# Scan inputs and output stage of a state-space network on Trainium2: the deltas by another route, and a longer pipeline

## The chip, the cores and the metric

The kernel runs on one core of one Trainium2 chip. The metric is the device time of one execution in microseconds (us). Three runs of the kernel before took 20491.51, 20492.61 and 20494.03 us; the median is 20492.61. A separate execution was recorded by the hardware profiler, and all rows in this document come from it.

## The reference

The program maps 32 images of 96 channels and 32 x 32 points (1024 points, HW below) through four layers. The change touches layers 0 and 1, both selective scans. From an inner signal u of 192 channels (in layer 1 four directions of it, 768 channels) a projection gives B and C (16 rows each) and a low-rank dt (6 rows), and dt gives a step size delta for every channel and point:

```python
x_dbl = xl @ W_x
dt_r = x_dbl[..., :dr]
Bm = x_dbl[..., dr:dr + n]
Cm = x_dbl[..., dr + n:]
delta = jax.nn.softplus(dt_r @ W_delta + b_delta)
...
dA = jnp.exp(dt[:, :, None] * A)
h = dA * h + (dt * u_t)[:, :, None] * B_t[:, None, :]
```

Layer 0 does the same forward and backward along sequences of 8 frames, with u made by a causal convolution of four taps and a SiLU. It then adds both directions, multiplies by a gate z, projects back to 96 channels, adds the input and normalises over the channels. Layers 2 and 3 (attention and a quantised feed-forward) are as they were.

## The kernel before, in words

The program is a row of stages with a barrier between them. Each stage is a function with its own buffers; it reads its inputs from HBM and writes its results there. Within a stage each engine has its own program, written out in the code, and runs it strictly in that order; semaphores say when an operand is ready. `nth(k)` is the value that a semaphore has once step k is done. `turns` unrolls four turns in a loop. So the order of the code is the order of the work, and a wait at the head of an engine holds everything behind it. Three functions matter.

`l0_scan_inputs` (line 292, run forward as `l0pf` and backward as `l0pb`) prepares the scans of layer 0. A turn handles two frames in three tiles of 128 rows by 1024 points. VectorE makes u by four taps (lines 415 and 419), TensorE projects u to 38 rows (`project`, lines 501 and 502), ScalarE copies them out (`read`, line 528), TensorE makes the deltas' argument x = W dt + b in PSUM tile `pd` (`deltas`, lines 487 and 490). The softplus is computed as max(x, 0) + ln(1 + exp(-|x|)): VectorE stores max(x, 0) in `dl` (line 437) and -|x| = x - 2 max(x, 0) in `ab` (line 440), ScalarE takes exponential and logarithm (546, 548), and GpSimd adds (line 391). A turn later VectorE multiplies delta by u (line 427), TensorE transposes the product in 8 blocks (466), and ScalarE copies that out (537). At the end of a turn ScalarE applies the SiLU, which needs another table (559, 540).

`l0_out_proj` (line 570, `l0out`) takes the images in pairs. For a pair, each step is done for both images before the next: VectorE adds the directions (624) and multiplies by z (629), TensorE projects (664), VectorE adds the input (636), TensorE averages (672), VectorE subtracts (642), ScalarE squares (694), TensorE averages (678), ScalarE takes logarithm and exponential (698, 702), VectorE scales and shifts (647, 650). All input buffers are double. SP loads image k once image k - 2 is out of its buffers, ScalarE's queue stores.

`l1_scan_inputs` (line 1148, `l1p`) does for layer 1 what the first function does for layer 0, an image a turn, in six tiles (three forward, three reversed). There is no convolution. The projection is one block of eight f32 matmuls of 512 columns in the second slot of a turn (`project`, line 1292), for the next image; deltas run two tiles ahead (1299), the product with u runs three tiles behind on VectorE (1271), the transposes four (1308), the copy out five (1354).

In the names of rows, `px` is the projection in PSUM, `dts` its copy, `pt` the transposed product and `dut` its copy, `bt` the transposed B.

Of the kernel before, what the change touches and what calls it, by code (L numbers as in the profile page):

```python
# [19 lines left out]
BF16 = mybir.dt.bfloat16  # L20
# [271 lines left out]
def l0_scan_inputs(nc, back, xmp, w, us, dls, duts, bts, crows, ident):  # L292
# [8 lines left out]

    with ExitStack() as stack:
# [19 lines left out]
        const, taps, conv, silu, xd, dtc, btm, btc, dtm, plus, absd, expd, lnd, sumd, dud, dutm, dutc, passed = r.step_sems(  # L322
            "const", "taps", "conv", "silu", "xd", "dtc", "btm", "btc", "dtm", "plus", "absd", "expd", "lnd", "sumd",
# [9 lines left out]
        with nc.Block() as block:  # L333
# [52 lines left out]
            @block.gpsimd  # L386
            def _(pool):
                def turn(k, s):
                    for t in range(T):
                        pool.wait_ge(lnd, nth(T * k + t))  # L390
                        pool.tensor_tensor(dl[:, s % 2, t, :], dl[:, s % 2, t, :], ln[:, t, :], ALU.add).then_inc(sumd, 1)

                turns(pool, turn, 0, 0, UNROLL, ITEMS)

            @block.vector
            def _(dve):
# [4 lines left out]
                def turn(k, s):  # L401
# [50 lines left out]
            def _(pe):  # L452
# [3 lines left out]
                def turn(k, s):  # L456
# [2289 lines left out]
```

## Time and profile before

| | |
|---|---|
| median of three runs | 20492.61 us |
| profiled execution | 20482.76 us |
| its span, first to last instruction | 20481.2 us |
| granted TensorE clock, mean over the span | 0.957 |
| TensorE matmul busy | 18308.0 us, 89% |
| VectorE busy | 17098.0 us, 83% |
| ScalarE busy | 15840.3 us, 77% |
| GpSimd busy | 13907.5 us, 68% |

The shares are averages over stages with different limits, so they do not tell what a change in one stage is worth. PE is TensorE (PEld its weight loads), DVE is VectorE, ACT is ScalarE, POOL is GpSimd, SP the engine that issues most DMAs.
### The profile page before, as it was taken

Reading aid. Unit: us, or ns where it says so; the run is one execution under the profiler, and the core shown is the slowest. Engines: PE = TensorE matmul, PEld = TensorE weight load, DVE = VectorE, ACT = ScalarE, POOL = GpSimd, SP = SyncE. Lnnn points to the kernel's source line nnn. Section 1 sums busy time; section 2 is a strip of 40 time slices with the busy share of each in tenths; the row PEclk is TensorE's granted clock in tenths of the full one; section 3 lists DMA queues with packets and bytes.
Section 4 is the critical chain, followed back from the end, with each engine's and each line's share of the span. In section 5 each row is a group of like instructions: output and inputs, shape, how many; then the busy total and the mean of one; then the engine's idle time right before and its main releaser. Section 6 shows DMA issues by size and latency. Waiting matters only on the chain. (4 is left out here: it accounts for less than half of the span.)

```text
span 20481.2 us, 269190 instructions
## 1 busy us (share of the span) xinstructions
PE 18308.0 (89%) x75272; PEld 10298.6 (50%) x75272; DVE 17098.0 (83%) x12555; ACT 15840.3 (77%) x24692; POOL 13907.5 (68%) x6884
## 2 busy tenths in 40 slices
PE   8799997999958899889899999999999999789798
PEld 3355553555523344335566666666666665245353
DVE  4899998899967499469899999999999999755666
ACT  7599995999934555567799999999999999234545
POOL 0399992899916488155599999999999999000101
PEclk9799997999989999999999999999999999799999
DMA  5688875888873411657633333333333333910303
GB/s 176 204 241 241 237 230 190 244 241 241 243 209 87 174 72 69 210 205 266 232 128 117 126 117 127 117 127 116 127 117 127 116 127 106 217 42 27 91 28 85
DMA packets 842574, 3172.29 MB, mean 155 GB/s; under 512 B 101542, under 2 KB 124682, under 8 KB 816140
## 3 DMA queue, kind: packets, MB, share of 16 engines
q1 hardware_dynamic: 820236, 3080.90, 47.0%
q10 hardware_dynamic: 20992, 75.51, 1.0%
q8 instruction: 593, 9.72, 0.2%
q14 instruction: 753, 6.17, 0.1%
HBM read 2317.15 MB, written 838.88 MB: 154 GB/s over the span
## 5 line engine op out<-in xcount | busy, mean ns | idle before, releaser
L1575 DVE TENSOR_TENSOR_SCAN l1s_h<-l1s_da,l1s_pd 128x1024 f32<-128x1024 f32 x3072 | 6818.6, 2273 | 329.2 <-PE l1s_pd L1510 246.3
L1613 ACT ACTIVATE l1s_dm<-l1s_dut,l1s_bt 128x384 f32<-128x384 f32 x7680 | 4182.5, 602 | 16.7 <-PE l1s_pd L1510 16.5
L1596 ACT ACTIVATE l1s_da<-l1s_dl,l1s_a 128x1024 f32<-128x1024 f32 x3072 | 3493.3, 1137 | 75.1 <-DVE l1s_h L1575 51.0
L1510 PE MATMUL l1s_pd<-l1s_id,l1s_dm 128*128 128x128 f32 x23040 | 3059.0, 275 | 159.9 <-DVE l1s_h L1575 116.1
L1510 PEld LDWEIGHTS l1s_pd<-l1s_id,l1s_dm 128*128 128x128 f32 x23040 | 2632.3, 142 | 826.8 <-issue 533.1
L1479 POOL TENSOR_TENSOR l1s_sm<-l1s_h 128x1024 f32<-128x1024 f32 x1024 | 2434.2, 2377 | 170.4 <-DVE l1s_h L1575 170.2
L1484 POOL TENSOR_TENSOR l1s_pb<-l1s_h,l1s_cc 128x1024 f32<-128x1024 f32 x1024 | 2436.5, 2379 | 1.0 <-DVE l1s_h L1575 0.3
L1488 POOL TENSOR_TENSOR l1s_pa<-l1s_sm,l1s_cc 128x1024 f32<-128x1024 f32 x1024 | 2433.6, 2377 | 0.0
L886 POOL TENSOR_TENSOR dw_acc<-dw_acc,dw_prod 128x961 f32<-128x961 f32 (+3 forms) x704 | 1573.2, 2281 | 1005.7 <-ACT dw_prod L839 997.5
L1520 PE MATMUL l1s_py<-l1s_pb,l1s_id 128*128 128x512 f32 x4096 | 2014.3, 614 | 215.2 <-POOL l1s_pb L1484 214.8
L2145 POOL CAST ffn_h<-ffn_z 128x1024 fp8e5<-128x1024 f16 x128 | 181.0, 1415 | 2894.7 <-DVE ffn_z L2165 2889.6
L1520 PE MATMUL l1s_py<-l1s_pa,l1s_id 128*128 128x512 f32 x4096 | 1927.4, 593 | 0.3 <-POOL l1s_pa L1488 0.3
L2400 POOL TENSOR_TENSOR l0sf_pr<-l0sf_h,l0sf_cc 128x1024 f32<-128x1024 f32 x768 | 1816.6, 2386 | 69.1 <-DVE l0sf_h L2482 51.1
L2400 POOL TENSOR_TENSOR l0sb_pr<-l0sb_h,l0sb_cc 128x1024 f32<-128x1024 f32 x768 | 1813.7, 2380 | 67.4 <-DVE l0sb_h L2482 60.6
L817 PE MATMUL dw_pc<-dw_vol,dw_diag 128*128 128x512 f32 (+7 forms) x4224 | 1765.1, 581 | 57.2 <-DMA dw_vol<-n 30.3
L916 DVE SCALAR_TENSOR_TENSOR dw_pc<-dw_vol,dw_wt,dw_pc 128x961 f32<-128x961 f32 (+5 forms) x1280 | 1484.6, 1234 | 210.0 <-PE dw_pc L817 206.0
L2438 PE MATMUL l0sf_py<-l0sf_pr,l0sf_id 128*128 128x512 f32 x3072 | 1578.6, 596 | 0.0
L2438 PE MATMUL l0sb_py<-l0sb_pr,l0sb_id 128*128 128x512 f32 x3072 | 1578.6, 596 | 0.0
L2530 ACT ACTIVATE l0sb_dm<-l0sb_dut,l0sb_bt 128x192 f32<-128x192 f32 x3584 | 1313.9, 443 | 9.4 <-DMA l0sb_dl<-l0dlsb 9.4
L2530 ACT ACTIVATE l0sf_dm<-l0sf_dut,l0sf_bt 128x192 f32<-128x192 f32 x3584 | 1312.1, 441 | 9.2 <-DMA l0sf_dl<-l0dlsf 9.2
L817 PEld LDWEIGHTS dw_pc<-dw_vol,dw_diag 128*128 128x128 f32 (+1 forms) x4224 | 774.8, 184 | 1047.6 <-issue 1031.3
L2418 PEld LDWEIGHTS l0sb_pd<-l0sb_id,l0sb_dm 128*128 128x128 f32 x6144 | 761.7, 142 | 929.3 <-issue 682.4
(300 smaller groups left out, 32080.3 us busy)
## 6 DMA issues: line engine op xcount, KB each, us to landing
l1s_cc<-crows SPq DMA_DIRECT2D x1024, 512.0 KB, 3.7
l0sf_cc<-l0crowsf SPq DMA_DIRECT2D x512, 512.0 KB, 5.8
l0sb_cc<-l0crowsb SPq DMA_DIRECT2D x512, 512.0 KB, 5.4
l0sf_cc<-l0crowsf SPq DMA_DIRECT2D x512, 256.0 KB, 7.7
l0sb_cc<-l0crowsb SPq DMA_DIRECT2D x512, 256.0 KB, 7.1
dls<-l1p_dl SPq DMA_DIRECT2D x192, 512.0 KB, 7.0
duts<-l1p_dut SPq DMA_DIRECT2D x64, 1536.0 KB, 5.8
l1s_dut<-duts SPq DMA_DIRECT2D x64, 1536.0 KB, 7.2
```

What stands on the lines that cost most here:

```text
L817: mm = pe.matmul(pixels(pc[:, f % 4, :])[:, ys, xs], diag[:, v % tiles, diag_taps.index(tap), :], source(v, f, tap, ys, xs), start=(n == 0 ...
L1479: pool.tensor_tensor(sm[:, rnd % 2, :], h[:, rnd * HT % 4, :], h[:, (rnd * HT + 1) % 4, :], ALU.add)\
L1484: pool.tensor_tensor(pb[:, rnd % 2, :], h[:, (rnd * HT + 2) % 4, :], cc[:, rnd % 4, :], ALU.mult)\
L1488: pool.tensor_tensor(pa[:, rnd % 2, :], sm[:, rnd % 2, :], cc[:, rnd % 4, :], ALU.mult)\
L1510: mm = pe.transpose(pd[:, s % 2, blk * 128:blk * 128 + 128], dm[:, rnd % 2, blk, j * 128:j * 128 + 128], idt[:, :])
L1520: mm = pe.matmul(target[:, hs], idt[:, :], prods[:, rnd % 2, hs], start=(n == 0), stop=(n == N - 1))
L1575: dve.tensor_tensor_scan(h[:, s % 4, :], da[:, j, :], pd[:, s % 2, :], 0.0, ALU.mult, ALU.add)\
L1596: act.activation(da[:, j, :], dl[:, half, j, :], ACT.Exp, scale=a[:, HT * half + j, n:n + 1])\
L1613: ins = act.activation(dm[:, rnd % 2, blk, :], dut[:, half, blk, :], ACT.Identity, scale=bt[:, half, blk, n:n + 1])
L2400: pool.tensor_tensor(pr[:, s % 4, :], h[:, s % 6, :], cc[:, rnd % 4, j, :], ALU.mult).then_inc(prod, 1)
L2438: mm = pe.matmul(py[:, j, HALVES[half]], idt[:, :], pr[:, s % 4, HALVES[half]], start=(n == 0), stop=(n == N - 1))
L2530: ins = act.activation(out, src, ACT.Identity, scale=b)
```

## The change

**Layer 0, scan inputs.** GpSimd's program is gone. VectorE computes -|x| in one operation, by setting the sign bit of x in PSUM, and no longer stores max(x, 0). The new last step `softplus` reads x again from PSUM and ln(1 + exp(-|x|)) from SBUF and gives max(x, 0) + ln(...) in one operation. It comes after the convolution tap of its slot, and the sign operation before the tap. TensorE makes the deltas one tile ahead. A buffer of `pd` is now free only once `softplus` has read it.

**Layer 0, output stage.** Input buffers are four deep, the stores are on SP, and the three parts of an image's chain are done in three successive turns, each engine working on images k, k + 1 and k + 2 in a turn.

**Layer 1, scan inputs.** The dt rows of the projection are made nine times (three groups of three copies); 128 output rows were computed before too, most of them zeros. ScalarE copies all 128 rows to bf16 (`parts`), VectorE subtracts to get what is left for 64 rows (`rest`), ScalarE rounds that to bf16, VectorE subtracts once more for 32 rows. So `parts` holds high, middle and low parts of dt, and W is split in three in the same way; one bf16 matmul with 128 rows of contraction gives the sum of the nine products. A bf16 row of ones adds the bias row by two more matmuls an image. B and C are copied apart (`bc`). The projection is in four pieces, spread over four slots. The product with u moves to GpSimd, the softplus is as in layer 0, and both VectorE operations on deltas are in two halves of 512 points with a semaphore step each.

```diff
 # l0_scan_inputs
-            @block.gpsimd
-            def _(pool):
-                def turn(k, s):
-                    for t in range(T):
-                        pool.wait_ge(lnd, nth(T * k + t))
-                        pool.tensor_tensor(dl[:, s % 2, t, :], dl[:, s % 2, t, :], ln[:, t, :], ALU.add).then_inc(sumd, 1)
...
+                            dve.wait_ge(dtm, nth(T * k + t))
+                            dve.wait_ge(expd, nth(T * (k - 1) + t))
+                            dve.tensor_scalar(ab[:, t, :].bitcast(I32), pd[:, (s + t) % 2, :].bitcast(I32), SIGN, None, ALU.bitwise_or).then_inc(absd, 1)
...
+                            dve.wait_ge(lnd, nth(T * k + t))
+                            dve.scalar_tensor_tensor(out=dl[:, p, t, :], in0=pd[:, (s + t) % 2, :], scalar=0.0, in1=ln[:, t, :],
+                                                     op0=ALU.max, op1=ALU.add).then_inc(sumd, 1)
...
                     for t in range(T):
                         times_u(t)
+                        minus_abs(t)
                         convolve(t)
-                        minus_abs(t)
+                        softplus(t)
                     convolve(3)
...
-                        pe.wait_ge(absd, nth(T * k + t - 2))
+                        pe.wait_ge(sumd, nth(T * k + t - 2))
...
                     for t in range(T):
+                        if t < T - 1:
+                            deltas(k, s, t + 1)
+                        else:
+                            deltas(k + 1, s + 1, 0)
                         turn_du(t)
-                        deltas(t)
                         if t < 2:
                             project(t)
 # l0_out_proj, VectorE
-                with dve.Fori(0, FRAMES) as c:
-                    for pair in pairs:
...
+                    if there(k1):
+                        dve.wait_ge(proj, nth(k1))
+                        dve.wait_ge(s_xm[s1 % 2], (k1 - s1 % 2) * 8)
+                        dve.tensor_tensor(xo[:, s1 % 2, :], xin[:, s1, :], po[:, s1 % 2, :], ALU.add).then_inc(resid, 1)
+                    if there(k2):
+                        dve.wait_ge(s_in[s2], c2 * 112 + 112)
...
 # l1_scan_inputs, GpSimd
+                            pool.wait_ge(sumd, nth(2 * q + 1))
+                            pool.wait_ge(dutm, nth(q - 2))
+                            pool.tensor_tensor(du[:, t % 2, :], dl[:, t, :], in_order(s, t), ALU.mult).then_inc(dud, 1)
 # VectorE
+                            for i, hs in enumerate(HALVES):
+                                dve.wait_ge(dtm, nth(2 * q + i))
+                                dve.tensor_scalar(ab[:, t % 3, hs].bitcast(I32), pd[:, t % 2, hs].bitcast(I32), SIGN, None,
+                                                  ALU.bitwise_or).then_inc(absd, 1)
...
+                        if t == 3 and there(k + 1):
+                            dve.wait_ge(hi, nth(k + 1))
+                            dve.wait_ge(mid, nth(k))
+                            dve.tensor_tensor(rest[GROUPS, :], px[GROUPS, :], parts[GROUPS, p, :], ALU.subtract).then_inc(res, 1)
+                        if t == 4 and there(k + 1):
+                            dve.wait_ge(mid, nth(k + 1))
+                            dve.tensor_tensor(parts[96:128, p, :], rest[96:128, :], parts[96:128, p, :], ALU.subtract)\
+                               .then_inc(lo, 1)
 # TensorE
+                        pe.wait_ge(lo, nth(m))
+                        for i, hs in enumerate(HALVES):
+                            pe.wait_ge(sumd, nth(2 * (T * m + v - 2) + i))
+                            mm = pe.matmul(pd[:, v % 2, hs], wdel[:, v, :], parts[:, (s + (t + 2) // T) % 2, hs],
 # ScalarE
+                        if t == 3 and there(k + 1):
+                            act.wait_ge(xd, nth(k + 1))
+                            act.wait_ge(dtm, nth(2 * (T * (k - 1) + T - 1) + 1))
+                            act.activation(parts[:, p, :], px[:, :], ACT.Copy).then_inc(hi, 1)
+                        if t == 4 and there(k + 1):
+                            act.wait_ge(res, nth(k + 1))
+                            act.activation(parts[GROUPS, p, :], rest[GROUPS, :], ACT.Copy).then_inc(mid, 1)
```

The order of TensorE's instructions in layer 1's scan inputs, before, from one image's projection on (`px` is the projection, `pt` the transposes, `pd` the deltas):

```order
L1292 MATMUL l1p_px<-l1p_u,l1p_wsum 128x512 x8
L1308 MATMUL l1p_pt<-l1p_id,l1p_du 128x128 x8
L1299 MATMUL l1p_pd<-l1p_dts,l1p_wd 128x512 x2
L1308 MATMUL l1p_pt<-l1p_id,l1p_du 128x128 x8
L1299 MATMUL l1p_pd<-l1p_dts,l1p_wd 128x512 x2
L1314 MATMUL l1p_px<-l1p_id,l1p_dts 128x16 x8
L1308 MATMUL l1p_pt<-l1p_id,l1p_du 128x128 x8
L1299 MATMUL l1p_pd<-l1p_dts,l1p_wd 128x512 x2
```

And after, from the deltas ahead of the second projection piece on:

```order
L1348 MATMUL l1p_pd<-l1p_parts,l1p_wdel 128x512 x2
L1357 MATMUL l1p_pt<-l1p_id,l1p_du 128x128 x8
L1338 MATMUL l1p_px<-l1p_u,l1p_wsum 128x512 x2
L1340 MATMUL l1p_px<-l1p_one,l1p_oneat 128x512
L1348 MATMUL l1p_pd<-l1p_parts,l1p_wdel 128x512 x2
L1357 MATMUL l1p_pt<-l1p_id,l1p_du 128x128 x8
L1338 MATMUL l1p_px<-l1p_u,l1p_wsum 128x512 x2
L1348 MATMUL l1p_pd<-l1p_parts,l1p_wdel 128x512 x2
L1357 MATMUL l1p_pt<-l1p_id,l1p_du 128x128 x8
L1338 MATMUL l1p_px<-l1p_u,l1p_wsum 128x512 x2
L1340 MATMUL l1p_px<-l1p_one,l1p_oneat 128x512
L1348 MATMUL l1p_pd<-l1p_parts,l1p_wdel 128x512 x2
```

The eight projection matmuls stood in one row; now two of them stand behind each of four transposes, and the deltas come ahead of the transposes.

ScalarE in the same stage, before, from the copy of the projection on (`dut` is the copy of the transposes, the two `ln` rows are exponential and logarithm):

```order
L1346 ACTIVATE l1p_dts<-l1p_px 38x1024
L1354 ACTIVATE l1p_dut<-l1p_pt 128x8x128
L1360 ACTIVATE l1p_ln<-l1p_ab 128x1024
L1362 ACTIVATE l1p_ln<-l1p_ln 128x1024
L1354 ACTIVATE l1p_dut<-l1p_pt 128x8x128
L1360 ACTIVATE l1p_ln<-l1p_ab 128x1024
L1362 ACTIVATE l1p_ln<-l1p_ln 128x1024
L1368 ACTIVATE l1p_bt<-l1p_px 128x128
```

And after, from the copy out ahead of that copy on:

```order
L1398 ACTIVATE l1p_dut<-l1p_pt 128x8x128
L1402 ACTIVATE l1p_parts<-l1p_px 128x1024
L1410 ACTIVATE l1p_ln<-l1p_ab 128x1024
L1412 ACTIVATE l1p_ln<-l1p_ln 128x1024
L1416 ACTIVATE l1p_bc<-l1p_px 32x1024
L1398 ACTIVATE l1p_dut<-l1p_pt 128x8x128
L1405 ACTIVATE l1p_parts<-l1p_rest 64x1024
L1410 ACTIVATE l1p_ln<-l1p_ab 128x1024
L1412 ACTIVATE l1p_ln<-l1p_ln 128x1024
L1398 ACTIVATE l1p_dut<-l1p_pt 128x8x128
L1410 ACTIVATE l1p_ln<-l1p_ab 128x1024
```

Three instructions of 1024 points stand where one stood, and the copy of B and C comes after the first tile's logarithm.

VectorE in layer 0's forward scan inputs, before, from the second slot's product on (`du` is the product with u, `u` the taps):

```order
L427 TENSOR_TENSOR l0pf_du<-l0pf_dl,l0pf_u 128x1024
L419 SCALAR_TENSOR_TENSOR l0pf_u<-l0pf_xb,l0pf_cw,l0pf_u 128x1024 x3
L437 TENSOR_SCALAR l0pf_dl<-l0pf_pd 128x1024
L440 SCALAR_TENSOR_TENSOR l0pf_ab<-l0pf_dl,l0pf_pd 128x1024
L427 TENSOR_TENSOR l0pf_du<-l0pf_dl,l0pf_u 128x1024
L419 SCALAR_TENSOR_TENSOR l0pf_u<-l0pf_xb,l0pf_cw,l0pf_u 128x1024 x3
L437 TENSOR_SCALAR l0pf_dl<-l0pf_pd 128x1024
L440 SCALAR_TENSOR_TENSOR l0pf_ab<-l0pf_dl,l0pf_pd 128x1024
L419 SCALAR_TENSOR_TENSOR l0pf_u<-l0pf_xb,l0pf_cw,l0pf_u 128x1024 x3
```

And after, from the same product on:

```order
L419 TENSOR_TENSOR l0pf_du<-l0pf_dl,l0pf_u 128x1024
L427 TENSOR_SCALAR l0pf_ab<-l0pf_pd 128x1024
L411 SCALAR_TENSOR_TENSOR l0pf_u<-l0pf_xb,l0pf_cw,l0pf_u 128x1024 x3
L435 SCALAR_TENSOR_TENSOR l0pf_dl<-l0pf_pd,l0pf_ln 128x1024
L419 TENSOR_TENSOR l0pf_du<-l0pf_dl,l0pf_u 128x1024
L427 TENSOR_SCALAR l0pf_ab<-l0pf_pd 128x1024
L411 SCALAR_TENSOR_TENSOR l0pf_u<-l0pf_xb,l0pf_cw,l0pf_u 128x1024 x3
L435 SCALAR_TENSOR_TENSOR l0pf_dl<-l0pf_pd,l0pf_ln 128x1024
L411 SCALAR_TENSOR_TENSOR l0pf_u<-l0pf_xb,l0pf_cw,l0pf_u 128x1024 x3
```

The sign operation (`ab`) has moved ahead of the taps, and what gives `dl` now reads `ln` and stands behind them.

## Rows read from the trace of the kernel before

**Rows 1.** Busy time by window, core 0: three changed stages, columns as in the first line
```profile
core 0: us, PE busy (x) PEld busy (x) DVE busy (x) ACT busy (x) POOL busy (x), PEclk, DMA share, GB/s
363.00:944.00 581.00, 385.19 (x1408) 195.36 (x1408) 473.47 (x340) 270.98 (x244) 112.55 (x48) 0.75 0.56 185
5725.00:6265.00 540.00, 276.93 (x512) 92.48 (x512) 288.58 (x260) 99.60 (x96) 0.00 (x0) 0.77 0.74 213
9187.00:10115.00 928.00, 806.79 (x3328) 460.80 (x3328) 787.94 (x587) 621.07 (x642) 456.85 (x192) 0.97 0.70 264
```

**Rows 2.** Timeline of VectorE, one turn, first layer: start us, us, engine, line
```profile
598.70 3.37 DVE L419 SCALAR_TENSOR_TENSOR l0pf_u<-l0pf_xb,l0pf_cw,l0pf_u 128x1024 f32<-128x1024 f32 x1
601.99 1.21 DVE L427 TENSOR_TENSOR l0pf_du<-l0pf_dl,l0pf_u 128x1024 f32<-128x1024 f32 x1
603.13 2.25 DVE L415 TENSOR_SCALAR l0pf_u<-l0pf_xb,l0pf_cw 128x1024 f32<-128x1024 f32 x3
607.71 1.23 DVE L437 TENSOR_SCALAR l0pf_dl<-l0pf_pd 128x1024 f32<-128x1024 f32 x1 [2.33 <-PE l0pf_pd L487]
...
611.24 5.84 DVE L419 SCALAR_TENSOR_TENSOR l0pf_u<-l0pf_xb,l0pf_cw,l0pf_u 128x1024 f32<-128x1024 f32 x3
```

**Rows 3.** Line 419, the convolution taps: duration ns min/median/max
```profile
L419 DVE SCALAR_TENSOR_TENSOR l0pf_u<-l0pf_xb,l0pf_cw,l0pf_u x144: 1269/1279/3452, 378.3 to 862.3; 128x1024 f32<-128x1024 f32 x144
```

**Rows 4.** Timeline of ScalarE in the same turn, and five turns later
```profile
602.10 2.77 ACT L559 ACTIVATE l0pf_u<-l0pf_u 128x3072 f32<-128x3072 f32 x1 [1.96 <-DVE l0pf_u L419]
606.18 1.02 ACT L537 ACTIVATE l0pf_dut<-l0pf_pt 128x1024 f32<-128x1024 f32 x1
...
766.69 2.77 ACT L559 ACTIVATE l0pf_u<-l0pf_u 128x3072 f32<-128x3072 f32 x1 [1.96 <-DVE l0pf_u L419]
```

**Rows 5.** Timeline of TensorE in the same turn
```profile
612.32 1.88 PE L487 MATMUL l0pf_pd<-l0pf_dts,l0pf_wd 128*128 128x512 f32 x4
...
620.66 1.97 PE L466 MATMUL l0pf_pt<-l0pf_id,l0pf_du 128*128 128x128 f32 x8 [2.91 <-DVE l0pf_du L427]
622.56 2.45 PE L490 MATMUL l0pf_pd<-l0pf_dts,l0pf_wd 128*64 128x512 f32 x8
```

**Rows 6.** DMA of the output stage, 5733 to 6264 us
```profile
DMA packets 32729, 113.09 MB, mean 213 GB/s; under 512 B 5152, under 2 KB 5152, under 8 KB 32728
```

**Rows 7.** Timeline of ScalarE, second layer's scan inputs
```profile
9605.39 1.06 ACT L1362 ACTIVATE l1p_ln<-l1p_ln 128x1024 f32<-128x1024 f32 x1
9609.43 1.02 ACT L1346 ACTIVATE l1p_dts<-l1p_px 38x1024 f32<-38x1024 f32 x1 [2.99 <-PE l1p_px L1292]
9610.36 1.00 ACT L1354 ACTIVATE l1p_dut<-l1p_pt 128x1024 f32<-128x1024 f32 x1
...
9663.76 1.02 ACT L1346 ACTIVATE l1p_dts<-l1p_px 38x1024 f32<-38x1024 f32 x1 [3.22 <-PE l1p_px L1292]
```

**Rows 8.** Groups of instructions, 9400 to 9910 us, same stage
```profile
L1242 POOL TENSOR_TENSOR l1p_dl<-l1p_dl,l1p_ln 128x1024 f32<-128x1024 f32 x113 | 269.5, 2385 | 238.8 <-ACT l1p_ln L1362 238.8
L1299 PE MATMUL l1p_pd<-l1p_dts,l1p_wd 128*128 128x512 f32 x452 | 215.0, 598 | 4.6 <-DVE l1p_ab L1265 4.6
L1271 DVE TENSOR_TENSOR l1p_du<-l1p_dl,l1p_u 128x1024 f32<-128x1024 f32 x113 | 200.9, 1778 | 32.5 <-PE l1p_pt L1308 32.5
L1292 PE MATMUL l1p_px<-l1p_u,l1p_wsum 128*128 128x512 f32 x304 | 133.6, 592 | 0.0
L1308 PE MATMUL l1p_pt<-l1p_id,l1p_du 128*128 128x128 f32 x899 | 118.4, 275 | 38.8 <-ACT l1p_dut L1354 38.8
```

**Rows 9.** The nearest one-record matmul with 512 columns (fp8)
```profile
L2237 PE MATMUL ffn_po<-ffn_h,ffn_w 128*96 128x512 fp8e5 x384 | 98.3, 394 | 3.7 <-DVE ffn_h L2186 2.4 <-ACT ffn_o L2270 1.3
```

**Rows 10.** Two-microsecond windows; the granted clock is PEclk
```profile
618.00:620.00 2.00, 0.00 (x0) 0.00 (x0) 1.97 (x3) 0.49 (x1) 0.00 (x0) 1.00 0.00 0
620.00:622.00 2.00, 1.34 (x7) 1.34 (x8) 2.00 (x3) 1.97 (x3) 0.27 (x1) 0.55 0.00 0
...
9212.00:9214.00 2.00, 2.00 (x8) 1.74 (x9) 0.00 (x0) 0.28 (x1) 0.00 (x0) 0.50 0.92 231
```

More of the change, by code:

```diff
@@ L300, in here @@
         return there(k, ITEMS)
+    SIGN = -2 ** 31
     with ExitStack() as stack:
@@ L652, in _ @@
+                cycles(dve, turn, 2)
             @block.tensor
@@ new lines, in average, with turn @@
+                def average(p, source):
+                    for hs in HALVES:
+                        mm = pe.matmul(pm[:, p, hs], avg[:, :], source[:, p, hs], start=True, stop=True)
+                    return mm
+                def turn(c, s):
+                    k = c * SEQS + s
+                    c1, s1, k1 = ahead(c, s, 1)
+                    c2, s2, k2 = ahead(c, s, 2)
+                    if there(k):
+                        pe.wait_ge(sqr, nth(k))
+                        average(s % 2, sq).then_inc(var, 1)
+                    if there(k1):
+                        pe.wait_ge(resid, nth(k1))
+                        pe.wait_ge(lnv, nth(k1 - 2))
+                        average(s1 % 2, xo).then_inc(mean, 1)
+                    if there(k2):
+                        pe.wait_ge(gate, nth(2 * k2 + 1))
+                        pe.wait_ge(resid, nth(k2 - 2))
+                        for hs in HALVES:
+                            for q in range(2):
+                                mm = pe.matmul(po[:, s2 % 2, hs], wo[:, q, :], z[:, s2, q, hs], start=(q == 0), stop=(q == 1))
+                        mm.then_inc(proj, 1)
@@ L713, in depthwise @@
+                cycles(act, turn, 2)
 def depthwise(nc, stage, rows, src, dst, taps_w, bias, ident, tiles, volumes, turns, deep, func):
@@ new lines, in turn @@
+                        m, v = back(k, t, 1)
+                        if there(m):
+                            q = T * m + v
+                            dve.wait_ge(s_dl[v], m * 16)
+                            dve.wait_ge(dud, nth(q - T))
+                            dve.wait_ge(lnd, nth(q))
+                            for hs in HALVES:
+                                dve.scalar_tensor_tensor(out=dl[:, v, hs], in0=pd[:, v % 2, hs], scalar=0.0,
+                                                         in1=ln[:, v % 3, hs], op0=ALU.max, op1=ALU.add).then_inc(sumd, 1)
@@ L1318, in turn @@
                     for t in range(T):
+                        m, v = back(k, t, -2)
+                        if there(m):
+                            deltas(m, v)
                         m, v = back(k, t, TURN)
```

362 lines of the change are left out of this document (171 added, 191 removed).

## The prediction

> **What bounds the kernel now.** I read the busy time by window first [rows 1], then, in each changed stage, the timelines of the engines that wait. The profiled execution took 20482.8 us (span 20481.2 and 1.6 around it), the runs' median is 20492.6. The change touches four of the program's stages: the first layer's scan inputs, forward and backward (581 us each; the backward one has the same busy times within 1 us, so one is shown), its output stage (540 us) and the second layer's scan inputs (928 us), 2630 us together. The stages run one after the other, so what a stage loses the program loses. What the scans beside them do is not touched.
>
> In the first layer's scan inputs VectorE is the bound, 473 us busy of 581 [rows 1], but not with its own work alone. A turn takes (766.69 - 602.10) / 5 = 32.9 us [rows 4]. In it VectorE waits 2.3 us for the first delta matmul [rows 2], and three times a tap of 1.27 us takes 3.4 [rows 2, 3]: each time while GpSimd runs the addition of line 391. That is 3 x 2.1 = 6.3 us a turn.
>
> In the output stage nobody is full: VectorE 289 us, TensorE 277, the DMA engines 74% of 540 [rows 1]. Two images go through a chain of eight steps, and the loads of the next two start late.
>
> In the second layer's scan inputs a turn (an image) takes (9663.76 - 9609.43) / 2 = 27.2 us [rows 7]. TensorE is busy 807 of 928 us at a granted clock of 0.97, VectorE 788 [rows 1]. ScalarE is not full, but stands 3.0 us an image before the projection's result [rows 7].
>
> **First layer's scan inputs.** GpSimd's 48 additions go, and with them the 6.3 us. VectorE keeps its count (three products, three sign operations instead of the clamp, three clamp-and-add instead of the old subtraction), each 1.14 us from start to start [rows 2]. Summed: 9 x 1.14 + 2.25 + 9 x 1.25 = 23.8 us a turn. The new last step of a tile waits for ScalarE's logarithm, in place of the old wait for the matmul. Counted from the end of the fourth tap: Silu to 2.8, table load and the first copy out to 5.1 [rows 4], exponential and logarithm (1.06 each, as in [rows 7]) to 7.3. VectorE arrives at 1.1 + 1.2 + 2.25 = 4.6, so it waits 2.7 us there. Behind it wait the next product and TensorE's third delta matmuls, which need the buffer: 8.6, plus 2.45 [rows 5], plus the transposes 1.0 give 12.1, copy out, exponential and logarithm give 15.3, VectorE's taps end at 14.5: a wait of 0.8. The third tile is late by 0.4 in the same way. 23.8 + 3.9 = 27.7 us against 32.9. 14 of the 16 turns have taps: 14 x 5.2 = 73 us, and I take 70 for each direction, **-140 us**. Bounds: no waits, 14 x 9.1 x 2 = -255; TensorE's steps in that chain at half clock (8 transposes took 1.97 us after an idle time of 2.9 [rows 5]), 3 us more a turn, -62. The value is near the end that the timeline gives step by step.
>
> **Output stage.** Loads now run four images deep and are issued as soon as a buffer is free, stores too on SP's queue: seven loads and two stores an image are 9 x 0.5 us of issue, little beside the image. An image's chain is spread over three turns, so VectorE's 289 us and TensorE's 277 [rows 1] lie side by side and beside the DMA. The DMA is then the bound: 0.74 x 540 = 400 us with all 16 engines busy [rows 1], for 113.09 MB [rows 6]. With some 15 us until the first image has arrived and 25 us for the last image's chain it is 440 us: **-100 us**. Bounds: 289 + 40 = 329 us if packets overlap better when queued (-210); and -40 if TensorE at half clock and the handshakes keep 15.6 us an image.
> The Trainium skill ("DMA: Bandwidth & Descriptors", Specifications) gives about 358 GB/s from HBM to a core; here 113.09 MB in 400 us are 283 GB/s, which no stage is bound to keep. By the page's figure the estimate would be 316 us of DMA and a sum 84 us lower; I keep the row.
>
> **Second layer's scan inputs.** Removed: on TensorE a tile's deltas in f32, 215.0 / 113 = 1.90 us [rows 8]; on VectorE the product with u, 1.78 us a tile, long because it collides with GpSimd [rows 8]. Added: the deltas as one bf16 pass. This trace has no bf16 matmul; the nearest is the fp8 one with 512 columns, 0.39 us [rows 9]; two in a row I take at 0.6, bounded by 0.4 (no fill) and 1.9 (no gain). GpSimd multiplies instead of adds, 2.39 us [rows 8] of some 4.2 a tile, and its inputs are ready a slot earlier than anyone needs them. ScalarE gets two instructions more an image, 128 and 64 rows by 1024, some 1.0 each like line 1346 [rows 7]. VectorE gets two of about 1.2, and its operations on deltas are split in halves: 0.6 to 0.7 each, so 1.3 for 1.2; if a half costs as much as a whole, 2.4, VectorE has 29 + 2.4 us an image and is the bound, 4 us an image slower (upper bound); if exactly half, VectorE has 17 us (lower bound).
> Per image VectorE has then 6 x 2.6 + 2.4 = 18 us, GpSimd 14.3, TensorE 7.0 for the projection (133.6 / 19), 6 x 1.05 for the transposes (118.4 / 113), 6 x 0.6 for deltas, about 19 with the rest; ScalarE 6 x 3.0 + 1.0 + 0.9 + 1.0 + 0.3 = 21. No engine holds 27.2. What holds is a loop: ScalarE's bf16 copy needs the last projection piece, that comes on TensorE behind the deltas of tile 4, these need VectorE's clamp-and-add of tile 2, and that needs ScalarE's logarithm of tile 2. Counted from its end: clamp-and-add 1.4, deltas 1.7, transposes 2.6, the piece (7.0 / 4) 4.5. ScalarE has one copy (1.0) for that time and waits 3.5 us, half a microsecond more than now. Then, three us a tile: copy 5.5, tile 3 to 7.6, copy of B and C 8.6, copy out and second copy 10.4, tile 4 12.5, tile 5 15.5, B 15.8, three tiles 24.7. In those three TensorE has 3.1 us a tile (deltas, transposes, a piece), slightly more than ScalarE: 25.0 us. So the image would win 2.2 us, 32 x 2.2 = 70 us, at full clock.
> But TensorE now has nothing from 4.5 to 8.8 (deltas of tile 5 wait for tile 3's sum), and until 16 only short work between waits. In the first layer the granted clock fell from 1.00 to 0.55 within two windows around an idle time of 2.9 us, and 8 transposes took 1.97 instead of 1.05; at this stage's own start it was 0.50, the lower level, even in a window filled with work, after the transposes of B [rows 5, 8, 10]. At 1.2 GHz the slots of tiles 4 and 5 give: B's transposes to 15, transposes of tile 1 at 18.0 where ScalarE wants them at 15.8 (2.2 us late), and the first projection piece 3.5 instead of 1.75 if the clock is not back yet. The image comes to 27.3 with the clock back before that piece, to 29.1 without. I take 28.2, 1.0 us more than now: **+30 us** (bounds -70 and +60).
> The Trainium skill ("TensorE: Matmul & The Clock Gate", Part 1: The HAM clock gate) says "the default state is throttled, and activity releases the throttle". That rule speaks against making TensorE's work shorter here; by it the stage gives the +30, by the clock of this stage's rows (0.97) it would give the -70. Rows 10 agree with the rule.
> Start of the stage: seven operations on 128x768 weights before the first matmul, 0.9 us each scaled from 1.2 for 1024 columns, of which the first image's load hides some: **+5 us**.
>
> **Sum.** -140 - 100 + 30 + 5 = -205 us against the profiled 20482.8, which is 9.9 us under the median; the same step from the median gives 20288 us.
>
> **The rivals.**
> A: TensorE keeps its upper clock in the second layer's stage. For it: 0.97 there now. Against: gaps of 4.3 us that it does not have now. -205 - 100 = -305, 20188 us.
> B: the two first-layer gains are half of what I say, since the logarithm and TensorE at half clock come later in each turn and the output stage stays at 15 us an image. For it: clocks of 0.75 and 0.77 there now [rows 1]. Against: both stages lose measured waits. -205 + 120 = -85, 20408 us.
> C, the slower side: in the second layer's stage TensorE stays at 1.2 GHz through whole images. Then its work is 14 (projection) + 12 (transposes) + 3.5 (deltas) + 4 (the rest) and the 5 us of waits: 38.5 us an image, 32 x 11.3 = +362, total +117, 20610 us. It decides once an image takes more than 27.2 + 240 / 32 = 34.7 us. Against it: with such a turn TensorE would work without gaps for more than 20 us, and wherever it did so here the clock went back up.
> D: a step does not do what it says: the halves cost as much as wholes (+4 us an image, -80 in all) or the loads are held back by SP's order of waits. Time 20450 us or so.
>
> **How the numbers follow.** Forecast 0.55, A 0.22, B 0.14, C 0.04, D 0.05. The low end reaches to A and a little beyond, since the output stage may gain more: 20175. The high end takes in B: 20405. A measurement of this kernel tells 0.2% (41 us) from no change. Faster: forecast, A, B and half of D, 0.93; same: 0.03; slower: C, 0.04.
>
> **What would show it.** In the first layer line 411's taps all near 1.27 us, turns near 28 us, and VectorE's waits on ScalarE's logarithm, the longest at the first tile. In the output stage a DMA share over 0.9 and 430 to 450 us. In the second layer turns of 27 to 29 us, ScalarE waiting 3.5 us before line 1402, the delta matmuls one record each, a granted clock of 0.7 to 0.85 with 0.5 in the slots after the last projection piece. A clock above 0.95 there and turns of 25 us mean A. A turn above 35 us means C. A first-layer turn above 30 us or an output stage above 490 us means that I misjudged what waits there.

## The result, and the profile after

The changed kernel takes 20264.39 us (median of 4 runs, 20256.15 to 20274.33) against 20493.32 for the kernel before on the same chip (20491.51 to 20512.64): a ratio of 0.9886, 95% interval 0.9869 to 0.9904, so 1.1% faster. The forecast was 20288 us. The profiled execution has a span of 20254.3 us, 226.9 less than before.

To see where they went, the spans are cut at the first weight load of every stage (each stage begins with its own loads, in the trace on line 84's queue), and a stage lasts until the next one's first load:

| stage | before | after | difference | predicted |
|---|---|---|---|---|
| first layer, scan inputs forward | 571.3 | 493.2 | -78.1 | -70 |
| first layer, scan inputs backward | 568.6 | 495.3 | -73.3 | -70 |
| first layer, output stage | 534.9 | 456.9 | -78.0 | -100 |
| second layer, scan inputs | 910.6 | 906.0 | -4.6 | +35 |
| all others | 17895.8 | 17902.9 | +7.1 | 0 |

The same three windows as in [rows 1], of the kernel after (those of before were cut 5 to 17 us wider than the stages in the table):

```profile
core 0: us, PE busy (x) PEld busy (x) DVE busy (x) ACT busy (x) POOL busy (x), PEclk, DMA share, GB/s
364.00:857.00 493.00, 358.11 (x1408) 179.03 (x1408) 381.26 (x338) 272.29 (x243) 0.00 (x0) 0.85 0.64 214
5584.00:6040.00 456.00, 288.94 (x512) 98.89 (x512) 288.85 (x259) 104.30 (x97) 0.00 (x0) 0.79 0.96 249
8960.00:9866.00 906.00, 720.65 (x3008) 475.29 (x3008) 575.38 (x848) 675.12 (x705) 453.49 (x192) 0.78 0.70 265
```

VectorE lost 92 us of busy time in the first stage, and the output stage's DMA share went from 0.74 to 0.96, both as foretold. In the third stage TensorE and VectorE lost work, ScalarE gained 54 us, the clock fell from 0.97 to 0.78, and the time stayed.

One turn of the first layer, VectorE's timeline, answers to [rows 2]:

```profile
604.96 1.23 DVE L435 SCALAR_TENSOR_TENSOR l0pf_dl<-l0pf_pd,l0pf_ln 128x1024 f32<-128x1024 f32 x1 [3.96 <-ACT l0pf_ln L548]
...
632.01 1.22 DVE L435 SCALAR_TENSOR_TENSOR l0pf_dl<-l0pf_pd,l0pf_ln 128x1024 f32<-128x1024 f32 x1 [2.84 <-ACT l0pf_ln L548]
...
635.41 3.67 DVE L411 SCALAR_TENSOR_TENSOR l0pf_u<-l0pf_xb,l0pf_cw,l0pf_u 128x1024 f32<-128x1024 f32 x3
639.37 1.22 DVE L435 SCALAR_TENSOR_TENSOR l0pf_dl<-l0pf_pd,l0pf_ln 128x1024 f32<-128x1024 f32 x1 [0.29 <-ACT l0pf_ln L548]
...
646.97 1.23 DVE L435 SCALAR_TENSOR_TENSOR l0pf_dl<-l0pf_pd,l0pf_ln 128x1024 f32<-128x1024 f32 x1 [0.52 <-ACT l0pf_ln L548]
```

Three taps now take 3.67 us where they took 5.84, and none of the 144 took over 1.29 (3.45 in [rows 3]). The three waits for the logarithm are 2.84, 0.29 and 0.52 us (the prediction's hand schedule had 2.7, 0.8 and 0.4). The turn is 632.01 - 604.96 = 27.05 us; in one of four or five turns the copy of B waits longer for TensorE at half clock, and it is 28.2 (the 3.96 above belongs to such a one).

The output stage: its DMA line (against [rows 6]) and the two longest waits of VectorE (in total, how often, the longest).

```profile
DMA packets 32820, 113.42 MB, mean 249 GB/s; under 512 B 5168, under 2 KB 5168, under 8 KB 32816
```
```profile
DVE l0out_xo L642 <- PE l0out_po L692: 86.2, 31, 5.5
DVE l0out_yf L646 <- DMA l0out_xin<-in_x: 64.0, 30, 15.2
```

The same bytes go at 249 GB/s, not 283, though the engines are 96% busy: a packet takes 0.96 x 456 us / 32820 = 13.3 ns of all 16 engines' time, where it took 0.74 x 540 us / 32729 = 12.2 ns.

The second layer's stage, one image, TensorE's timeline and then ScalarE's (against [rows 7]):

```profile
9403.11 1.88 PE L1338 MATMUL l1p_px<-l1p_u,l1p_wsum 128*128 128x512 f32 x4
9404.83 0.38 PE L1340 MATMUL l1p_px<-l1p_one,l1p_oneat 128*128 128x512 bf16 x1
9409.63 1.21 PE L1348 MATMUL l1p_pd<-l1p_parts,l1p_wdel 128*128 128x512 bf16 x2 [4.42 <-DVE l1p_dl L1308]
9410.63 1.91 PE L1357 MATMUL l1p_pt<-l1p_id,l1p_du 128*128 128x128 f32 x8
9412.33 3.43 PE L1364 MATMUL l1p_px<-l1p_id,l1p_bc 128*128 128x16 f32 x16
...
9421.20 1.88 PE L1338 MATMUL l1p_px<-l1p_u,l1p_wsum 128*128 128x512 f32 x4
9422.92 0.59 PE L1348 MATMUL l1p_pd<-l1p_parts,l1p_wdel 128*128 128x512 bf16 x2
```
```profile
9400.29 1.02 ACT L1398 ACTIVATE l1p_dut<-l1p_pt 128x1024 f32<-128x1024 f32 x1 [0.18 <-PE l1p_pt L1357]
9405.25 1.02 ACT L1402 ACTIVATE l1p_parts<-l1p_px 128x1024 bf16<-128x1024 f32 x1 [3.94 <-PE l1p_px L1340]
9406.17 1.05 ACT L1410 ACTIVATE l1p_ln<-l1p_ab 128x1024 f32<-128x1024 f32 x1
```

It reads as a ring. ScalarE waits 3.94 us for the projection's last piece, so tile 3's exponential starts at 9406.17; VectorE's clamp-and-add comes behind it, at 9408.88; TensorE's next deltas wait 4.42 us for that, and everything from 9409.63 to 9421.20 runs at half clock (a bf16 pair 1.21 for 0.59, eight transposes 1.91 for 1.04). The clock is back exactly before the first projection piece. Two windows, before the gap and behind it (columns as above):

```profile
9402.00:9406.00 4.00, 3.21 (x15) 1.69 (x13) 0.00 (x0) 0.75 (x1) 3.04 (x2) 1.00 0.52 206
...
9414.00:9418.00 4.00, 4.00 (x19) 3.45 (x18) 2.85 (x5) 2.44 (x4) 1.00 (x1) 0.50 1.00 381
```

A turn, from the first and last of 32 such copies:

```profile
L1402 ACT ACTIVATE l1p_parts<-l1p_px x32: 1023/1023/1024, 8982.4 to 9814.9; 128x1024 bf16<-128x1024 f32 x32
```

is (9814.9 - 8982.4) / 31 = 26.85 us. Before, the copies of line 1346 had the same spacing:

```profile
L1346 ACT ACTIVATE l1p_dts<-l1p_px x32: 1017/1018/1022, 9209.6 to 10042.9; 38x1024 f32<-38x1024 f32 x32
```

(10042.9 - 9209.6) / 31 = 26.88. So the turns took as long as before. The first copy comes 22.4 us after the stage's first load, where it came after 18.9; the 31 turns together are 0.8 us shorter; and the next stage's first load comes 51.1 us after the last copy, where it came after 58.4. That makes the difference of 4.6 us.

### The profile page after: what moved, and what is told of

Read it like the earlier page. It is cut to its first block and busy times, and to the rows that moved or that the text cites. A ratio compares the mean times of both kernels' runs of the same rounds, so it can differ in the third digit from the quotient of the medians.

```text
span 20254.3 us, 269190 instructions
## 1 busy us (share of the span) xinstructions
PE 18187.5 (90%) x74952; PEld 10291.5 (51%) x74952; DVE 16703.4 (82%) x12821; ACT 15900.7 (79%) x24757; POOL 13677.2 (68%) x6788
```

## The experiments

Single profiled runs are compared stage by stage. In the first layer's scan inputs (492.4 to 497.1 us) and the second layer's (906.0 to 910.5 us), where no edit touches them, that is good to some 5 us. The exception is the output stage, whose code is the same in nine of the profiles (the changed kernel, experiments 1 to 5 and 8 below, and both runs of 9): it took 440 to 458 us in them, 451 in the middle. Nothing of less than 20 us can be read from it.

### 1. Second layer: the bf16 copy behind tile 3

```diff
-  (ScalarE, t == 3, ahead of the exponential)  wait xd; parts <- px
+  (ScalarE, t == 3, behind the logarithm)      wait xd; parts <- px
-  VectorE: rest at t == 3, lo at t == 4
+  VectorE: rest at t == 4 behind softplus, lo at t == 5 ahead of it
```

> The changed kernel, but in the second layer's scan inputs ScalarE's bf16 copy of the projection stands behind the exponential and logarithm of tile 3, not ahead of them; VectorE's two remainders follow it by one slot. Theory (the wait of ScalarE for the projection holds tile 3, that holds softplus of tile 3, and TensorE then idles 4.4 us an image with the clock falling to 1.2 GHz): the 4.4 us gap is gone or under 1.5 us, granted clock of the stage 0.76 rises to over 0.9, a turn goes from 26.85 to 22-24 us, the stage from 906 to 740-810 us. Rival (another loop sets the turn, the copy chain only moves its wait to the half-speed transposition of B): the turn stays 26-27.5 us, the stage 890-920.

Measured: stage 806.3 us for 906.0, the whole program 20148.68 us. The turn is (9701.2 - 8967.1) / 31 = 23.68 us. The copies' line, then TensorE and ScalarE around the same place:

```profile
L1412 ACT ACTIVATE l1p_parts<-l1p_px x32: 1024/1024/1025, 8967.1 to 9701.2; 128x1024 bf16<-128x1024 f32 x32
...
9389.79 0.38 PE L1340 MATMUL l1p_px<-l1p_one,l1p_oneat 128*128 128x512 bf16 x1
9390.00 0.59 PE L1348 MATMUL l1p_pd<-l1p_parts,l1p_wdel 128*128 128x512 bf16 x2
9393.08 1.09 PE L1357 MATMUL l1p_pt<-l1p_id,l1p_du 128*128 128x128 f32 x8 [2.48 <-ACT l1p_dut L1398]
```
```profile
9390.20 1.02 ACT L1412 ACTIVATE l1p_parts<-l1p_px 128x1024 bf16<-128x1024 f32 x1 [1.90 <-PE l1p_px L1340]
```
```profile
8945.00:9750.00 805.00, 646.41 (x2953) 413.49 (x3008) 577.64 (x848) 672.30 (x705) 482.39 (x192) 0.84 0.79 298
```

The 4.42 us gap is gone and with it 100 us: the ring was real. But TensorE's longest gap did not fall below 1.5 us, as I had expected it to; one of 2.48 us for another copy of ScalarE took its place, and the clock rose only to 0.84, not to over 0.9.

### 2. Second layer: deltas in float32 in the new order

```diff
-  parts (bf16, three groups of rows), rest, lo; deltas = wdel (bf16) x parts
+  dts (f32), one copy of 38 rows;               deltas = wd (f32) x dts
-  one_at x one_row behind each half of the projection
```

> The changed kernel, but in the second layer's scan inputs the deltas come from one float32 copy of the projection, as in the kernel before (no bf16 parts, no remainders, no row of ones), all else and the whole order as after. Theory (the stacked bf16 deltas save TensorE time, 0.59 against about 1.0 us a pair at full clock, 1.21 against about 1.9 at half, but cost ScalarE 1.05 and VectorE 2.45 us an image which lie in the same chain): the stage changes little, 895-935 us against 906. Rival (the bf16 form is what brought the clock's gain in the stage): stage over 950 us. Rival 2 (the chain of parts is what holds it): stage under 880 us.

Measured: stage 1021.6 us, 116 more than after and 111 more than before; the program 20367.12. The time is the first rival's: bf16 carries the stage. Its reason, that bf16 brought a gain of the clock, is not what the run shows, since the clock is higher with f32 deltas. The window of the stage, and two of TensorE's instructions:

```profile
8956.00:9976.00 1020.00, 852.05 (x3328) 483.94 (x3328) 502.97 (x774) 616.28 (x641) 452.80 (x192) 0.93 0.60 236
```
```profile
9403.62 3.50 PE L1319 MATMUL l1p_pd<-l1p_dts,l1p_wd 128*128 128x512 f32 x4 [4.03 <-DVE l1p_dl L1289]
9406.96 1.04 PE L1328 MATMUL l1p_pt<-l1p_id,l1p_du 128*128 128x128 f32 x8
9412.89 1.98 PE L1319 MATMUL l1p_pd<-l1p_dts,l1p_wd 128*128 128x512 f32 x4 [0.51 <-DVE l1p_dl L1289]
...
9417.30 1.88 PE L1319 MATMUL l1p_pd<-l1p_dts,l1p_wd 128*128 128x512 f32 x4
```

Here the clock is 0.93 and the stage is the slowest of all. A gap of 4.03 us is in it as well, but the clock is back after one pair of f32 deltas (3.50 us), where the bf16 kernel works at half for 11.6 us. Over the stage that is, estimated from the windows' clocks, 2 x (1 - 0.93) x 1020 / 32 = 4.5 us an image at half clock against 2 x (1 - 0.78) x 906 / 32 = 12.5. So in this stage two effects nearly cancel. All of the change but the bf16 form (the pieces, the new places of the operations, the ring that comes with them) costs 111 us, and the bf16 form gives 116 back. At full clock its deltas save 1.88 - 0.59 = 1.29 us a tile, 7.7 us an image; 116 / 32 = 3.6 of these show. Where the rest went no run shows; the longer time at half clock and the ring are the likely places.

### 3. First layer: GpSimd kept busy beside the new order

```diff
+  GpSimd: wait lnd; ja <- jb[0] + jb[1]      (scratch, 128x1024, after every logarithm)
```

> The changed kernel with one addition in both scan-input stages of the first layer: after every logarithm GpSimd adds two scratch buffers of its own (128x1024 float32, nothing reads the result), so the addition that the change took from GpSimd is there again as a load on the memory, not as a step of the chain. Theory (what the first layer gained is above all VectorE's taps that no longer run beside a GpSimd addition): taps of 3.4 us come back, each stage goes from 493-495 to 550-580 us. Rival (the gain is the shorter chain and the deltas a tile ahead): some taps are long again but each stage stays under 515 us.

Measured: 522.7 and 525.0 us, 30 more each: neither side (the program 20318.79). Two neighbours on VectorE, and then the line of the taps:

```profile
604.43 4.63 DVE L425 SCALAR_TENSOR_TENSOR l0pf_u<-l0pf_xb,l0pf_cw,l0pf_u 128x1024 f32<-128x1024 f32 x3
...
617.48 2.25 DVE L433 TENSOR_TENSOR l0pf_du<-l0pf_dl,l0pf_u 128x1024 f32<-128x1024 f32 x1
```
```profile
L425 DVE SCALAR_TENSOR_TENSOR l0pf_u<-l0pf_xb,l0pf_cw,l0pf_u x144: 1268/1272/2248, 377.5 to 811.5; 128x1024 f32<-128x1024 f32 x144
```

No tap reached 3.4 us; the longest took 2.25, and the products with u took it instead (2.25 for 1.21). GpSimd's addition starts with the softplus, which reads PSUM and stays at 1.21, so only its second half meets an operation with two SBUF inputs. In the forward stage the taps gain 13 us of busy time and the products 34, and the wait for the logarithm loses 16: that is the 30. A collision is priced by what stands beside it, which differs by order.

### 4. First layer: deltas a tile ahead, undone

```diff
-  deltas(t + 1); turn_du(t)
+  turn_du(t); deltas(t)
```

> The changed kernel, but in the first layer's scan inputs TensorE issues the deltas of a tile behind the transposition of the same tile's inputs, in the slot where the kernel before had them. Theory (a VectorE that isn't stretched any more would wait for softplus, since exponential and logarithm then start only after the deltas): VectorE's wait of 2.8 us a turn grows to 8-12 us, each stage goes from 493-495 to 570-650 us. Rival (the collision was all there was to gain): each stage under 515 us.

Measured: 644.6 and 642.5 us, 151 and 147 more, the whole program slower than before (20541.26). The theory's side, at its upper end. VectorE now waits where it reads the deltas, 224.7 us in 16 turns, some 14 a turn for the 8 to 12 expected:

```profile
L427 DVE TENSOR_SCALAR l0pf_ab<-l0pf_pd 128x1024 int32<-128x1024 int32 x48 | 58.8, 1225 | 224.7 <-PE l0pf_pd L484 150.3 <-PE l0pf_pd L487 74.3
```

### 5. First layer: deltas a tile ahead, and nothing else

```diff
   (TensorE as after: deltas(t + 1); turn_du(t))
-  VectorE: sign or; softplus = max(pd, 0) + ln
+  VectorE: dl = max(pd, 0); ab = -2 dl + pd;   GpSimd: dl += ln
```

> The changed kernel, but in the first layer's scan inputs only the order of TensorE is that of after (deltas a tile ahead); the maximum, the combination by -2 and GpSimd's addition are those of the kernel before. Theory (VectorE's waits for the deltas, 72 us a stage in the kernel before, go, and the taps of 3.4 us stay, or more of them are hit): each stage 571 falls to 500-530 us. Rival (what is waited for comes back as taps held up by GpSimd, or as a wait for its addition): over 555 us.

Measured: 512.4 and 505.6 us, the program 20270.38. The theory held. VectorE's groups, here:

```profile
L420 DVE SCALAR_TENSOR_TENSOR l0pf_u<-l0pf_xb,l0pf_cw,l0pf_u 128x1024 f32<-128x1024 f32 x144 | 252.4, 1809 | 0.0
...
L438 DVE TENSOR_SCALAR l0pf_dl<-l0pf_pd 128x1024 f32<-128x1024 f32 x48 | 58.2, 1212 | 15.9 <-PE l0pf_pd L489 13.1 <-PE l0pf_pd L492 2.7
```

in the kernel before (the taps' group) and in the kernel after:

```profile
L419 DVE SCALAR_TENSOR_TENSOR l0pf_u<-l0pf_xb,l0pf_cw,l0pf_u 128x1024 f32<-128x1024 f32 x144 | 265.5, 1900 | 0.0
```
```profile
L411 DVE SCALAR_TENSOR_TENSOR l0pf_u<-l0pf_xb,l0pf_cw,l0pf_u 128x1024 f32<-128x1024 f32 x144 | 175.7, 1279 | 0.0
L435 DVE SCALAR_TENSOR_TENSOR l0pf_dl<-l0pf_pd,l0pf_ln 128x1024 f32<-128x1024 f32 x48 | 58.8, 1224 | 88.2 <-ACT l0pf_ln L548 88.2
```

The four forward stages make a table: old softplus 571.3 behind and 512.4 ahead, new softplus 644.6 behind and 493.2 ahead. The deltas ahead are worth 59 us with the old softplus and 151 with the new; the new softplus costs 73 alone and brings 19 with them (backward 63, 147, 74 and 10). "New softplus" is more than one operation here: GpSimd's addition is gone, the sign operation stands ahead of the tap and no longer behind it, and `pd` is free only after the last step. Which of the three costs the 73 no run separates; the place of the sign operation is an untested rival, since VectorE then comes to the deltas a slot of taps earlier. From experiment 5 to after, the taps lose 77 us of busy time and the products 9, while the waits go from 16 us for the deltas to 88 for the logarithm, 72 more.

### 6. Output stage: a fifth of the bytes left out

```diff
-  each load: z[:, s] <- zs        (all images)
+  only in the first four images
```

> The changed kernel, but the first layer's output stage loads the gate z only for its first four images; the 28 later pairs of loads are left out (the later images are multiplied by what stands in the buffer). That takes about 22 of the stage's 113 MB. Theory (the stage is bound by its transfers, whose engines are 97% busy): it falls from 440-457 us to 350-380. Rival (the chain between VectorE, TensorE and ScalarE sets it, and the queues are merely kept full): over 425 us.

Measured: 417.9 us, with 90 MB (the program 20215.10). Between the two sides: 33 us less than the middle of 451, where a stage bound by bytes would lose 20% of it, 90.

```profile
5577.00:5994.00 417.00, 295.61 (x512) 99.65 (x512) 286.58 (x259) 103.72 (x97) 0.00 (x0) 0.78 0.85 219
```

The DMA share falls to 0.85 and the rate to 219 GB/s. VectorE's waits for loads fall from 64.0 us in 30 times to 19.2 in 3, and its wait for TensorE's projection stays:

```profile
DVE l0out_xo L644 <- PE l0out_po L695: 90.7, 31, 7.0
```

So with fewer bytes the chain over VectorE and TensorE holds the stage, at little less than the transfers do.

### 7. Output stage: loads four images ahead, old order

```diff
-  yf, yb, z, xin: 2 buffers; loads of image k wait for image k - 2
+  4 buffers; loads of image k + 4 issued when image k is gated and added
   (pairs of images, stores by ScalarE: as before)
```

> The changed kernel, but the first layer's output stage has the order of the kernel before (pairs of images, stores issued by ScalarE) with four input buffers, so that each image's loads are issued four images ahead, as soon as its buffer is free, and not two. Theory (what was missing were transfers in flight, 74% busy before): the stage takes 440-475 us, as with the whole change. Rival (the order in pairs, whose waits for each other make a turn, sets it): 500-535 us, as in the kernel before.

Measured: 472.8 us, as the theory had it (the program 20259.13). The loads ahead give 62 us of the 84 that lie between 534.9 and 451; some 22 are left for the new order, little more than the 18 by which the stage scatters.

```profile
5582.00:6054.00 472.00, 257.79 (x512) 88.99 (x512) 290.32 (x258) 99.60 (x96) 0.00 (x0) 0.79 0.86 240
```

### 8. Second layer: the transposed tile first

```diff
   (experiment 1)
-  ScalarE: parts <- px; bc <- px; dut <- pt
+  ScalarE: dut <- pt; parts <- px; bc <- px
```

> The copy of the projection behind tile 3's logarithm, as in the run before, and ScalarE's copy of the last transposed tile moved from behind the copies of the projection to ahead of them, into its wait of 1.9 us. Theory (in that run TensorE still idled 2.5 us an image for this copy and the clock fell again): TensorE's longest wait is under 1.5 us, the granted clock of the stage 0.86 rises to over 0.93, the turn goes from 23.7 to 22.0-22.8 us, the stage from 806 to 755-785, the kernel to 20105-20140. Rival (ScalarE, 21 us of work a turn, and its next wait set it already): stage 795-815 us, kernel 20140-20165.

Measured: stage 793.8 us, a turn 23.3, the kernel 20142.54 (5 runs, 20129.27 to 20159.65; ratio to before 0.9829, 0.9815 to 0.9842). The stage gained 12 us, not 20 to 50: it lies just under the rival's 795 to 815, and the kernel's time is in the rival's range. The gap of 2.48 is gone, but two others are there, one over the 1.5 us expected, and the clock of the stage is 0.86, not over 0.93:

```profile
9418.64 1.04 PE L1357 MATMUL l1p_pt<-l1p_id,l1p_du 128*128 128x128 f32 x8
9420.84 1.93 PE L1364 MATMUL l1p_px<-l1p_id,l1p_bc 128*128 128x16 f32 x16 [1.16 <-DVE l1p_rest L1317]
9424.73 0.61 PE L1348 MATMUL l1p_pd<-l1p_parts,l1p_wdel 128*128 128x512 bf16 x1 [1.96 <-DVE l1p_dl L1312]
```
```profile
8956.00:9749.00 793.00, 635.61 (x2953) 406.96 (x3008) 575.50 (x848) 676.33 (x705) 453.62 (x192) 0.86 0.80 303
```

ScalarE has 676 of 793 us now, 21.1 of a turn of 23.3, more than any other engine.

### 9. First layer: a product put into the wait, then the logarithm first

```diff
   (experiment 8)
-  VectorE: softplus(0); times_u(1)
+  VectorE: times_u(1); softplus(0)
```

> The kernel with ScalarE's copy of the second layer moved (both moves), and in the first layer's scan inputs VectorE's product with tile 1 (1.2 us) placed ahead of softplus of tile 0, where VectorE waits 2.8 us a turn for the logarithm behind the SiLU. Theory (after the change the turn is VectorE's work and this wait, so work put into the wait shortens the turn by its length): the wait falls to 1.7 us, the turn by 1.1, each stage from 493 to 474-480 us. Rival (the wait is one side of a loop over TensorE and ScalarE, of which 3.3 and 3.0 us of ScalarE's waits for transposed tiles are the other): each stage 489-496.

Measured: 493.1 and 493.0 us for 492.8 and 492.6, the rival's side (the program 20119.65, the output stage being 12 us shorter in this run). Tile 0's and tile 1's waits:

```profile
603.33 1.22 DVE L435 SCALAR_TENSOR_TENSOR l0pf_dl<-l0pf_pd,l0pf_ln 128x1024 f32<-128x1024 f32 x1 [1.71 <-ACT l0pf_ln L552]
...
610.69 1.22 DVE L435 SCALAR_TENSOR_TENSOR l0pf_dl<-l0pf_pd,l0pf_ln 128x1024 f32<-128x1024 f32 x1 [1.43 <-ACT l0pf_ln L552]
```

The first wait fell from 2.84 to 1.71 as computed, and the second rose from 0.29 to 1.43: the sum is the same. The turn is not VectorE's work and its waits added up, since work put into the wait did not shorten it. It reads as a ring from tile 0's logarithm over softplus, TensorE and ScalarE to tile 1's.

```diff
   (the same)
-  ScalarE: copy of transposed tile 0; exponential, logarithm of tile 0
+  ScalarE: exponential, logarithm of tile 0; copy of transposed tile 0
```

> As the run before, and on ScalarE the exponential and logarithm of tile 0 stand ahead of the copy of the first transposed tile (1.0 us). Theory: VectorE's wait for tile 0 falls by another 0.9 us, the turn to 24.8-25.5 us, each stage to 455-468 us, the kernel to 20070-20100. Rival (the later copy holds TensorE's next transposition and the chain comes back there): each stage as in the run before, 474-480, or above.

Measured: 478.1 and 478.3 us, 15 less each, and the kernel 20100.76 (5 runs, 20075.82 to 20112.09; ratio to before 0.9813, 0.9800 to 0.9827). Direction right, size below the 25 to 38 expected. By its number 478 lies in the rival's 474 to 480, but that was meant as no gain over the run before, which took 493; neither side came as stated. The two waits are 1.11 and 1.43 now:

```profile
604.62 1.23 DVE L435 SCALAR_TENSOR_TENSOR l0pf_dl<-l0pf_pd,l0pf_ln 128x1024 f32<-128x1024 f32 x1 [1.43 <-ACT l0pf_ln L553]
...
623.71 1.22 DVE L435 SCALAR_TENSOR_TENSOR l0pf_dl<-l0pf_pd,l0pf_ln 128x1024 f32<-128x1024 f32 x1 [1.11 <-ACT l0pf_ln L553]
...
631.08 1.23 DVE L435 SCALAR_TENSOR_TENSOR l0pf_dl<-l0pf_pd,l0pf_ln 128x1024 f32<-128x1024 f32 x1 [1.43 <-ACT l0pf_ln L553]
```

The ring's own link was shortened, so the turn moved: 631.08 - 604.62 = 26.5 us for 27.05. This is the fastest version tried. Each measured beside its own runs of the kernel before, it stands at 0.9813 and the changed kernel at 0.9886, so it is some 0.7% or 150 us faster.

## Why the prediction was right

The forecast of 20288 us was 24 us too high. The changes in the first layer were seen in kind and size, that of the second layer's stage not in sign, and the terms were less near than their sum: in the profiles the first layer gained 11 us more than forecast and the second layer's stage 40 more, the output stage gained 22 less and the rest lost 7. That 29 of the 51 cancel is luck.

**First layer's scan inputs, -140 predicted, -151 measured: right in size, and the steps held.** The taps lost 265.5 - 175.7 = 90 us a stage where the sum had 14 x 6.3 = 88, and the waits on the logarithm came where they were computed. What the sum did not say is how its parts hang together. It treated the collisions as the greater part of the gain, 6.3 of the 9.1 us a turn from which the waits were then taken off. Experiment 5 shows that the order of TensorE alone brings 59 of the 78 us with 36 of the 42 long taps still there and four long products beside them, and experiment 4 that the new softplus, in its new place, costs 73 without it. What the taps gain by GpSimd's absence is nearly paid back in waits for the logarithm.

**Output stage, -100 predicted, -78 measured (-84 by the middle of the nine profiles): the mechanism was right, the term too large.** The step that was mis-sized is "0.74 x 540 = 400 us with all 16 engines busy": it holds the time of a packet fixed. Busy at 0.96 the engines moved 249 GB/s, so it takes 0.96 x 456 = 438 us of them, not 400. Experiment 6 shows that the chain is not far below either.

**Second layer, +35 predicted with its start, -5 measured: the term that was mis-sized.** The hand schedule was right in its instants: ScalarE's wait 3.94 for 3.5, TensorE's gap 4.42 for 4.3, half clock until the first projection piece. The step "the image comes to 27.3 with the clock back before that piece, to 29.1 without. I take 28.2" chose the middle of two cases; the trace has the first, with 26.85 for its 27.3. So 1.0 us an image too much, 32 us, is the mis-sized term; the start, 5 us in the sum, is the 3.5 us by which the first copy comes later; and the end of the stage, 7.3 us shorter, stood in no term. The difference of 4.6 is no more than what the same code shows between profiles. And the direction of the argument was incomplete: experiment 2 shows a stage at 0.93 clock that takes 116 us more. The short deltas were worth their price even at half clock. Rival A, the upper clock kept, did not come either; its 100 us were there to be had, though: experiment 1 took them by moving one copy, with the clock at 0.84. The prediction leaned on the Trainium skill ("TensorE: Matmul & The Clock Gate", Part 1: The HAM clock gate), by which the throttled state is the default and activity releases it. The first half fits this trace: 1.00 before the gap of 4.42 us, in which TensorE did nothing, and 0.50 behind it. The second half alone does not size the stage: TensorE worked almost without a pause from 9409.63 to 9421.20 and stayed at 0.50. Nor is less work by itself what took the clock from 0.97 to 0.78, since experiment 1 has the same work at 0.84.

**The rest, 0 predicted, +7 measured**, 14 of it after the second layer's scans, in stages that the change doesn't touch and that differ by as much between the runs of one kernel. It isn't explained.

Rivals B, C and D did not come: no first-layer turn above 30 us, no image above 34.7; two halves take 1.29 us for 1.2. Two of their sums are off as written: C's parts give +127 and 20620 us, not +117 and 20610, and D's -80 would be 20413 us, not 20450.

## What to carry to other kernels

When a wait moves from one instruction to its neighbour and the turn stays, you are in a ring, and only its own links help: put the ring's next step ahead of everything that can wait (a copy out, another tile's copy), on whichever engine it stands. Price a reordering and a new operation together, not one by one: here one edit was worth 59 or 151 us, and the other +73 or -19, depending on its partner. And do not size a transfer-bound stage by its busy share at an unchanged rate: here 213 GB/s at 0.74 became 249 at 0.96, not 276, and why a packet took longer no run shows.

## What the runs showed of the hardware that was not expected

- After a gap of about 4 us the granted clock fell in both forms of the second layer's stage, but one pair of 128x512 f32 deltas (3.50 us) was followed by full clock, where bf16 pairs, transposes and 16-column matmuls went on at half for 11.6 us. No run changed the kind of instruction behind a gap and nothing else, so that it is the kind that decides is not shown.
- B's transposition, 8 f32 matmuls (16 records) of 16 columns, took 3.43 us at half clock (the changed kernel) and 1.93 to 2.06 at mostly full clock (experiments 8 and 1), as much as four f32 matmul records of 512 columns (1.88).
- Beside a GpSimd addition (2.35 to 2.61 us) VectorE's product of two SBUF tiles took 2.25 us for 1.21; softplus, with one input in PSUM, stayed at 1.21.
- A 1024-column operation on VectorE cut in two halves took 1.29 us for 1.22:

```profile
9407.56 1.29 DVE L1299 TENSOR_SCALAR l1p_ab<-l1p_pd 128x512 int32<-128x512 int32 x2
```
